# A decoder layer on one Trainium2 core: Vector engine work moved at two places of a batch row, ranking sums taken inside the comparisons, and the experts' rectified values placed 64 bytes further

## What is computed

```python
x = _layernorm(x + _L0_attn_ref(x, ...))        # self attention, 16 heads, three branches
x = _layernorm(x + _L0_xattn_ref(x, ctx, ...))  # cross attention, 16 heads of 16
x = _layernorm(x + _L0_ffn_ref(x, ...))         # 8 experts, top 2, hidden size 1024
```

```python
scores = (x @ w_imp)[..., 0]
_, idx = jax.lax.top_k(scores, KEEP)      # KEEP = 64
idx = jnp.sort(idx, axis=1)
sel = jnp.take_along_axis(x, idx[:, :, None], axis=1)
```

## Time and profile before

| | |
|---|---|
| median of 3 runs | 1820.86 us (1814.07 to 1821.07) |
| profiled execution | 1819.49 us, its span 1817.6 us |
| mean granted PE clock | 0.991 of full speed |
| PE busy | 1734.4 us (95%) |
| DVE busy | 1272.2 us (70%) |
| ACT busy | 881.9 us (49%) |
| POOL busy | 1041.7 us (57%) |

### The profile page before, as it was taken

One profiled execution on the slowest core, in us unless ns is written; L12 is line 12 of the kernel. 1 busy time (PEld: TensorE's weight loads), 2 busy tenths in 40 slices (PEclk: granted clock), 3 DMA queues, 4 the chain that ended last, 5 costly groups with the idle time before them and its releaser, 6 DMA issues. The chain is left out here.

```text
span 1817.6 us, 34047 instructions
## 1 busy us (share of the span) xinstructions
PE 1734.4 (95%) x11512; PEld 1347.4 (74%) x11512; DVE 1272.2 (70%) x4111; ACT 881.9 (49%) x2827; POOL 1041.7 (57%) x1451
## 2 busy tenths in 40 slices
PE   7899999999999999999999879999999999999998
PEld 4575665765765765756756648999899989998997
DVE  4668878878877878877788657756655575657556
ACT  1565856846846937847758663221322132213221
POOL 2454654745745836736646556765766476648553
PEclk9999999999999999999999989999999999999999
DMA  5000000000000000000000101100010101010001
GB/s 174 7 1 8 7 8 7 2 8 7 2 8 7 2 8 7 2 7 8 2 8 2 48 1 70 48 1 23 25 47 1 47 1 47 1 47 1 1 1 47
DMA packets 24670, 33.91 MB, mean 19 GB/s; under 512 B 5104, under 2 KB 20976, under 8 KB 24368
## 3 DMA queue, kind: packets, MB, share of 16 engines
q1 hardware_dynamic: 24496, 31.73, 5.3%
HBM read 29.62 MB, written 2.10 MB: 17 GB/s over the span
## 5 line engine op out<-in xcount | busy, mean ns | idle before, releaser
L1985 POOL TENSOR_TENSOR h_lo<-h_sb,h_hi 128x512 fp32r<-128x512 f32 x256 | 362.8, 1445 | 111.8 <-DVE h_hi L2160 111.8
L2031 ACT ACTIVATE h_sb<-ps_H,b_sb 128x512 f32<-128x512 f32 x256 | 176.6, 690 | 508.8 <-PE ps_H L2199 481.9
L634 POOL TENSOR_TENSOR pr<-pr,rden 128x128 f32<-128x128 f32 (+2 forms) x768 | 307.8, 435 | 120.4 <-DVE rden L1199 120.3
L2160 DVE CAST h_hi<-h_sb 128x512 fp32r<-128x512 f32 x256 | 236.2, 937 | 134.4 <-ACT h_sb L2031 134.2
L839 ACT ACTIVATE pr<-sm,nmx 128x128 f32<-128x128 f32 (+2 forms) x768 | 311.6, 410 | 36.8 <-DVE nmx L1218 36.6
L2199 PE MATMUL ps_Y<-w_lo,h_hi 128*128 128x256 f32 x1024 | 287.8, 281 | 0.0
L2199 PE MATMUL ps_Y<-w_hi,h_lo 128*128 128x256 f32 x1024 | 287.6, 281 | 0.0
L2199 PE MATMUL ps_Y<-w_hi,h_hi 128*128 128x256 f32 x1024 | 287.6, 281 | 0.0
L669 POOL TENSOR_TENSOR pr<-pr,rden 128x256 f32<-128x256 f32 x256 | 151.1, 612 | 185.0 <-DVE rden L1199 185.0
L1210 DVE CUSTOM_DVE_ANT_0 sm<-ps_S,cmask 128x128 f32<-128x128 f32 (+2 forms) x768 | 191.7, 308 | 36.0 <-PE ps_S L1408 19.5
L2199 PE MATMUL ps_H<-x_hi,w_hi 128*128 128x512 f32 x512 | 199.5, 390 | 1.9 <-POOL w_lo L676 1.9
(11 more groups left out here) (245 smaller groups left out, 3383.6 us busy)
## 6 DMA issues: line engine op xcount, KB each, us to landing
w_raw<-in_W SPq DMA_DIRECT2D x16, 1024.0 KB, 6.3
xin<-in_x SPq DMA_DIRECT2D x8, 256.0 KB, 3.1
cin<-in_ctx SPq DMA_DIRECT2D x8, 256.0 KB, 2.6
w_kw<-in_wink SPq DMA_DIRECT2D x2, 768.0 KB, 6.5
w_ks<-in_selk SPq DMA_DIRECT2D x2, 768.0 KB, 9.8
out<-x SPq DMA_DIRECT2D x3, 512.0 KB, 3.4
b_sb<-in_b SPq DMA_DIRECT2D x1, 1024.0 KB, 4.3
w_qd<-in_dq SPq DMA_DIRECT2D x1, 576.0 KB, 4.6
```

Source lines behind the costliest of these rows:

```text
L634: last = pool.tensor_tensor(p_, p_, rden[:, h % 2, n:n + 1].to_broadcast([P, width]), ALU.mult)
L1985: pool.tensor_tensor(h_lo[:, s % 2, ht, :], h_sb[:, ht % 4, :], h_hi[:, s % 2, ht, :].bitcast(F32), ALU.subtract).then_inc(lo_sb.sem, 1)
L2031: ins = act.activation(h_sb[:, ht % 4, :], pst[plan.bank(f)][:, :], ACT.Relu, bias=b1[:, 2 * i + s // NCH, ht:ht + 1])
L2160: dve.tensor_copy(h_hi[:, s % 2, ht, :], h_sb[:, ht % 4, :]).then_inc(hi_sb.sem, 1)
```

## The change

Four edits, all on DVE's queue or in the placement of tensors.

1. `own_scores` takes the diagonal with two instructions that multiply and sum at once (`tensor_tensor_reduce` with `accum_out`); the separate sum goes. `beaten_by` sums each mask while it writes it (`accum_out` into the new tensors `above` and `level`); the rank is then one addition of two 128x2 tensors instead of an addition and a sum over 128x512. `FRONT_STEPS` counts the two instructions that are gone. The two new tensors take 64 bytes each, so what lies behind them in the attention stage moves by 128 bytes.
2. `rope_products(1, 0)` moves from behind a `yield` to in front of it: on DVE it now comes before row `i`'s evacuation of `kx` and `vx`, which the `interleave` puts there.
3. At `h == NH + 1` and `NH + 2` the reciprocals of the next row's head 0 move from behind `scores(following, 1)` to behind the next step's `turn_probs_x(15)`, and before `scores(following, 2)`.
4. The spacer grows from 8 to 24 floats, so `h_hi` and `h_lo` lie 64 bytes further.

```diff
-FRONT_STEPS = 28
+FRONT_STEPS = 26
...
+        above, level = sb("above", [P, NT]), sb("level", [P, NT])
...
                     for t in range(NT):
-                        dve.tensor_tensor(cmp1[:, t, 0:P], srow[:, P * t:P * t + P], ident[:, :], ALU.mult
-                                          ).then_inc(c.step(), 1)
+                        dve.tensor_tensor_reduce(out=cmp1[:, t, 0:P], in0=srow[:, P * t:P * t + P], in1=ident[:, :],
+                                                 scale=1.0, scalar=0.0, op0=ALU.mult, op1=ALU.add,
+                                                 accum_out=scol[:, t:t + 1]).then_inc(c.step(), 1)
                     dve.wait_ge(c.sem, c.value())
-                    dve.tensor_reduce(scol[:, :], cmp1[:, :, 0:P], AX, ALU.add).then_inc(c.step(), 1)
-                    dve.wait_ge(c.sem, c.value())
 
                 def beaten_by(t):
-                    dve.tensor_scalar(cmp1[:, t, :], srow[:, :], scol[:, t:t + 1], None, ALU.is_gt
-                                      ).then_inc(c.step(), 1)
+                    dve.tensor_scalar(cmp1[:, t, :], srow[:, :], scol[:, t:t + 1], 0.0, ALU.is_gt, ALU.add,
+                                      accum_out=above[:, t:t + 1]).then_inc(c.step(), 1)
                     dve.scalar_tensor_tensor(cmp2[:, t, :], srow[:, :], scol[:, t:t + 1], tie[:, t, :],
-                                             ALU.is_equal, ALU.mult).then_inc(c.step(), 1)
+                                             ALU.is_equal, ALU.mult, accum_out=level[:, t:t + 1]).then_inc(c.step(), 1)
...
                 dve.sem_inc(lat_sb.sem, 1)
-                yield
-
                 rope_products(1, 0)
+                yield
+
                 rope_products(1, 1)
                 yield
...
                 dve.wait_ge(c.sem, c.value())
-                dve.tensor_tensor(cmp1[:, :, :], cmp1[:, :, :], cmp2[:, :, :], ALU.add).then_inc(c.step(), 1)
-                dve.wait_ge(c.sem, c.value())
-                dve.tensor_reduce(rank[:, :], cmp1[:, :, :], AX, ALU.add).then_inc(c.step(), 1)
+                dve.tensor_tensor(rank[:, :], above[:, :], level[:, :], ALU.add).then_inc(c.step(), 1)
...
-                    if following is not None and h >= NH:
+                    if following is not None and h == NH + 1:
+                        scores(following, 1)
+                    elif following is not None and h == NH + 2:
+                        denominators(following, 0, 0, 6)
+                        scores(following, 2)
+                        denominators(following, 1, 1, 6)
+                    elif following is not None and h >= NH:
                         head_step(following, h - NH)
...
-        sb("half_line", [P, LINE // 8])
+        sb("half_line", [P, 24])
```

More of the change, by code:

```diff
@@ L1109, in front @@
                 dve.sem_inc(lat_sb.sem, 1)
+                rope_products(1, 0)
                 yield
-                rope_products(1, 0)
                 rope_products(1, 1)
```

## The result

The changed kernel takes 1801.41 us, the median of 5 runs (1800.14 to 1804.59). The kernel before took 1820.86 us beside it (5 runs, 1814.07 to 1823.86). The ratio is 0.9907, interval 0.9889 to 0.9926: faster by 0.9%, more than the 0.5% that can be told from nothing. Forecast were 1807 us, range 1799 to 1816.

A forecast was written before the change was run, and what follows sets the result against it. PE was taken to bound the kernel, with ACT tight in the heads. Seven passes of 0.95 + 0.55 + 0.33 = 1.83 us are 12.8, with front 0 13.2, from 1819.5 to 1806.3, plus 1.4: 1807 us, range 1799 to 1816.

The forecast's parts named there:

- Edit 2, 0.95 a pass: PE's key product behind the rotary products: moving them earlier on DVE saves 0.95 us a pass, bounds 0.75 and 0.95.
- edit 2's 0.95 comes on top and is not eaten here: At the own scores: their chain starts with a copy waiting for PE, so the rotary gain adds in full.
- Edit 1, own scores: DVE's own scores before key_turn: 1.26 us becomes 0.21 + 0.4 = 0.6, saving PE 0.65 us.
- The comparisons: DVE's four comparisons with sums attached: 0.26 us more together (0.18 to 0.34), about 0.1 reaching PE.
- The rival of the half pace: Summed comparison with two SBUF inputs takes a second cycle per element: 0.53 us more a pass, time 1811; chance 0.07.
- The rank: DVE's rank falls from 1.43 to some 0.2 us, worth nothing in a pass because DVE then waits for PE.
- Edit 1 net: 0.55 forecast: Own scores net of the slower comparisons: 0.55 us gained a pass.
- the pass gains what ACT gains: 0.33: Copy before reciprocal at the row seam: PE 0.46 us sooner, but ACT is tight, so 0.33 (0.2 to 0.46).
- The sum of a pass: Attention pass: 0.95 + 0.55 + 0.33 = 1.83 us gained, 12.8 over seven passes.
- the rival in which the gain is handed back: PE comes earlier and stands at its next wait; only the rotary product's gain counts, 1814 us; chance 0.17.
- the stage's pace shows no trace of another engine's accesses. I cost it at nothing: Experts: moving h_hi and h_lo 64 bytes keeps their position in a 64-byte line and gains nothing.
- The rival that priced a placement as half or double of 8.7 ns: Experts' output products: new place doubles the 8.7 ns fixed cost, 1834 us, or halves it, 1794; chance 0.05 each.

The follow-up runs named there:

- e1_sums: Kernel before with only the summed own scores, summed comparisons and short rank; 1812.3 us.
- e3_quiet_96: Kernel before with h_hi and h_lo 64 bytes further, DVE and POOL writing one column instead of 512 in some experts' turns; 1814.5 us.
- e2_line: Changed kernel with a spacer of 16 floats instead of 24, h_hi and h_lo at 64 bytes modulo 128; 1802.0 us.
- quiet pair: Kernel before, h_hi and h_lo at 32 or 96 bytes modulo 128, DVE's or POOL's writes to them cut in some turns; 1819.3 and 1814.5 us.

## Why the prediction was right, and where it was not

The direction and the range held; the forecast lay 5.6 us above the result. Its last sum has a slip: 1806.3 and 1.4 are 1807.7, not 1807. Point by point:

- **Edit 2, 0.95 a pass: right in mechanism, 0.86 measured,** between its bounds of 0.75 and 0.95. "edit 2's 0.95 comes on top and is not eaten here" failed by a little: 0.15 us of each came back at `key_turn`, because the own scores now meet more of POOL's normalising (1.44 us instead of 1.26). `kx` never became a wait.
- **Edit 1, own scores: the size of a term was wrong.** 1.26 us was to become 0.6 and became 1.01, 0.82 in e1_sums. The 0.21 us for the 128-element form, start to start, was taken from a place where its input is in PSUM, and it holds here with both inputs in SBUF: 0.20 in front 0. The wait for the sum was 0.50, not 0.4. What the term left out is POOL, which normalises beside the pair: the first takes 0.57 us in place of 0.28, 0.39 without edit 2. So PE's wait behind `key_turn` is 0.5 us each time, where 0.1 to 0.3 was to be seen. The Trainium skill, page SBUF — State Buffer, section Who interferes with whom, says that DVE's second pair of SBUF ports is GpSimd's, and that whoever has it locks the other out; the trace agrees, the 0.57 us ending 0.14 us after POOL's work does. That POOL is the cause is shown by the counts: 0.28 us in all 118 cases without it, and an end tied to POOL's in 93 of 106 with it. That it acts through the ports is the page's account, and no run here tells it from another lock between the two.
- **The comparisons: right.** 0.29 us more for 0.26 expected, 0.11 of it reaching PE for 0.1. The rival of the half pace falls, with 474 ns beside 472. The Trainium skill, page Vector Engine (DVE) Microarchitecture Reference, section Points that are easy to get wrong, has this kind at half throughput with two SBUF sources that are not bf16. The trace does not bear that out: the comparison with one source and a sum takes 464 ns, and half its pace would be some 0.27 us more, by the prediction's price for 256 elements.
- **The rank: right that it is worth nothing,** by a different way: `sel` ends with POOL's sum as it did before, so it takes up most of the freed time. For front 0, 0.4 us was taken; the scatter of 2.3 us hides it.
- **Edit 1 net: 0.55 forecast, 0.36 measured.**
- **Edit 3: "the pass gains what ACT gains: 0.33" failed.** The pass gained 0.45, PE's whole 0.46 and the upper bound. That an engine works almost without a gap did not make it the bound: PE's wait fell by 3.1 us in seven passes, and no wait for ACT or POOL took its place.
- **The sum of a pass: 1.83 forecast, 1.68 measured.** The single edits give 0.86 + 0.36 + 0.45 = 1.67, so they add up and the rival in which the gain is handed back falls. That 1.83 is so near is in part luck: edit 3's term was 0.12 too small, and those of edits 1 and 2 were 0.19 and 0.09 too large. The seven passes shrank by 13.3 us between the two profiled executions, and by 12.2 between e3_quiet_96 and e2_line, which have the two kernels' attention code and no clock drop; 12.8 was forecast.
- **Edit 4: "the stage's pace shows no trace of another engine's accesses. I cost it at nothing" is the step that failed most.** It gave 3.7 us, two thirds of the miss. The reasoning was about other engines, and the quiet pair bears it out that they have no part, but it left out PE's own reading of its stationary operand, whose place moved. That a pace is the same step after step says that nothing disturbs it, not that it is the best pace. The rival that priced a placement as half or double of 8.7 ns had the kind of effect right and the size wrong: 11.36 to 11.27 us is 0.9 ns a product.

## What to carry to other kernels

A stall of PE that DVE's order causes is worth nearly its whole length when what is moved behind has cover. Take the price of a DVE instruction from a row with the same neighbour on POOL, and ask which POOL instruction an earlier start will meet: edit 2 lost 0.18 us of DVE's time that way. Where one engine is the whole chain for hundreds of microseconds, try other addresses for its operands, here four in steps of 32 bytes: it costs one spacer, and a trace shows a hundredth of a microsecond that the times can't. Carry a reordering that works at one place to its siblings and run it: here it gave some 0.3 us a pass more, against my own odds. Before a sum over passes is credited to a change, look at the granted clock in each of them.

## What the runs showed of the hardware that I had not expected

- 96 products of 256 columns take 11.51, 11.36, 11.31 or 11.27 us with the stationary operands at 0, 32, 64 or 96 bytes modulo 128; at 32 and 96 it is the same with hardly any writes to them. At 0 the weight loads take 192 ns instead of 188.
- A DVE product of 128 elements a partition with two SBUF inputs took 0.28 us without POOL. Started during a POOL instruction it took 0.39 or 0.57, and ended 0.14 to 0.15 us after that. A DVE comparison of two elements with one SBUF input took 0.40 or 1.17 us and ended 0.02 to 0.03 us after POOL's sum each time.
- A comparison with a single input pays 126 ns for its sum (338 to 464), one with two inputs 2 ns (472 to 474).
- PE's granted clock fell to 0.50 for some 3 us inside a busy stretch and cost 1.0 to 1.5 us; it happened in none, one or two of an execution's seven passes, not always the same, and always 63 to 65 us behind the pass's residual.
